# Six half-bank output slots, straight-line code and a third index buffer in the edge loop of a graph layer on Trainium2

## What is computed

```python
def reference(x, src, dst, edge_weight, ...):          # x [6250, 256], 100000 edges sorted by dst
    xn = layernorm(x)
    agg = segment_sum(edge_weight[:, None] * xn[dst], src, 6250)
    x = x + (agg @ gnn_W.T + gnn_b) + linear_attention(xn)
    h = layernorm(x)
    for e in range(8):                                  # top 2 of 8 experts, softmax of their scores
        out += combine[:, e] * (relu(h @ W1[e].T + b1[e]) @ W2[e].T + b2[e])
    return x + out
```

## Time and profile before

| | before |
|---|---|
| device time, 3 runs | 2444.96 to 2448.07 us, median 2445.28 |
| the profiled execution | 2440.68 us, span of its instructions 2438.9 us |
| mean granted TensorE clock | 0.824 of full speed |
| PE busy | 1657.1 us (68%) |
| DVE busy | 1435.1 us (59%) |
| ACT busy | 1321.6 us (54%) |
| POOL busy | 1394.9 us (57%) |
| the edge loop: first to last gather | 327.0 to 1687.9 us |

### The profile page before, as it was taken

The page is one execution under the profiler, slowest core; times in us unless marked ns, Lnnn a source line. Parts: engine busy times, 40 slices in busy tenths (PEclk is TensorE's granted clock), DMA queues, the critical chain, the costliest instruction groups (busy, mean ns, idle before and its releaser), DMA issues. The chain is left out here.

```text
span 2438.9 us, 52037 instructions
## 1 busy us (share of the span) xinstructions
PE 1657.1 (68%) x13448; PEld 1188.0 (49%) x13448; DVE 1435.1 (59%) x3494; ACT 1321.6 (54%) x4250; POOL 1394.9 (57%) x1333
## 2 busy tenths in 40 slices
PE   6876446666666566666665444444639999999998
PEld 3465424444444445545442111122327777777776
DVE  7998535555555565555555554555855555555554
ACT  6454335555555455555555555554645665666665
POOL 3688846666666666666666666665404444444444
PEclk8999868888888687888986656566559999999999
DMA  4022144444444443333333334442612233233222
GB/s 145 15 85 71 55 130 133 131 125 131 129 126 128 132 118 101 99 99 99 101 90 90 88 89 119 148 136 77 205 26 43 48 50 49 45 50 49 46 49 32
DMA packets 139601, 224.62 MB, mean 92 GB/s; under 512 B 33398, under 2 KB 94016, under 8 KB 139298
## 3 DMA queue, kind: packets, MB, share of 16 engines
q0 software_dynamic: 67040, 146.22, 23.5%
q1 hardware_dynamic: 66022, 69.75, 9.6%
q10 hardware_dynamic: 6364, 6.40, 0.8%
HBM read 181.40 MB, written 41.82 MB: 92 GB/s over the span
## 5 line engine op out<-in xcount | busy, mean ns | idle before, releaser
L961 POOL DMA_INDIRECT misc<-z_d,consts x902 | 861.0, 955 | 520.0 <-remote 251.1
L1206 DVE SCALAR_TENSOR_TENSOR acc<-ps,consts,acc 128x256 f32 x902 | 434.2, 481 | 545.6 <-remote 485.4
L1286 PE MATMUL ps<-misc 128*128 128x256 f16 x565 | 185.5, 328 | 295.4 <-DVE acc L1206 150.0
L1790 ACT ACTIVATE misc<-ps,misc 128x128 f32<-128x128 f32 x840 | 240.1, 369 | 237.8 <-PE ps L1755 166.1
L985 ACT ACTIVATE rec<-rec,misc 128x128 f16<-128x128 f16 x674 | 229.2, 392 | 210.8 <-DVE rec L1067 145.3
L1831 POOL DMA_INDIRECT out<-misc,pos x105 | 166.2, 1583 | 289.0 <-ACT misc L1855 253.3
L1755 PE MATMUL ps<-misc,big 128*128 128x128 f16 x1680 | 327.2, 220 | 0.0
L1753 PE MATMUL ps<-misc,big 128*128 128x128 f16 x1680 | 326.8, 220 | 0.1
L1754 PE MATMUL ps<-misc,big 128*128 128x128 f16 x1680 | 326.5, 219 | 0.0
L985 ACT ACTIVATE misc<-rec,misc 128x128 f16<-128x128 f16 x678 | 229.1, 391 | 171.6 <-DVE rec L1067 128.2
L1770 PE MATMUL ps<-big,rec 128*128 x840 | 319.7, 381 | 0.0
(11 more groups left out here) (336 smaller groups left out, 3835.6 us busy)
## 6 DMA issues: line engine op xcount, KB each, us to landing
big<-in_w2T SPq DMA_DIRECT2D x60, 256.0 KB
misc<-z_d,consts POOLq DMA_INDIRECT x902
big<-xT_d SPq DMA_DIRECT2D x98, 128.0 KB
big<-in_w1T SPq DMA_DIRECT2D x32, 256.0 KB
tok_d<-misc SPq DMA_DIRECT2D x50, 132.0 KB, 2.8
xT_d<-misc SPq DMA_DIRECT2D x49, 128.0 KB
z_d<-misc SPq DMA_DIRECT2D x49, 128.0 KB
acc<-in_x SPq DMA_DIRECT2D x1, 6144.0 KB
```

Source lines behind the costliest of these rows:

```text
L961: e.indirect_dma_start(out=rows[k], out_offset=None, in_=c.z_d, in_offset=bass.IndirectOffsetOnAxis(ap=idx[u][:, k:k + 1], axis=0)).then_i ...
L1206: e.scalar_tensor_tensor(out=rows_of, in0=out_ps[t % BG], scalar=c.gain, in1=rows_of, op0=ALU.mult, op1=ALU.add).then_inc(s_add[k], 1)
L1286: e.matmul(o, w[:, 0, :], rows[k][:, 0:D], start=True, stop=False)
L1790: l = e.activation(hidden[:, m, :], h_ps[u][:, m, :], ACT.Relu, bias=b1x[u][:, m:m + 1])
```

## The change

Three edits, all in `graph`. **Slots:** `BG` goes from 3 to 6, and two tiles share a bank, each in one half; PE and DVE now wait once for two tiles. PE asks before an even tile t for the addition of tile t-5 (so both tiles that had the bank before are added), and DVE asks before it adds an even tile t for the product of tile t+1. **Straight line:** PE, ACT and DVE run `for at in range(LOOPS)`, with no loop of the sequencers and constants in all counts. **Third buffer:** `idx` and `near` have three buffers, and `fetch` copies round q+2 while ACT is in round q; rounds 0 and 1 are copied before the first turn.

```diff
-UG, HG, OG, BG, LEAD = 12, 8, 4, 3, 6
+UG, HG, OG, BG, LEAD = 12, 8, 4, 6, 6
...
-        c.idx = [k.take(UG, I32) for _ in range(2)]
+        c.idx = [k.take(UG, I32) for _ in range(3)]
...
-    near = [matrix(misc.take(UG * 3), UG, 3) for _ in range(2)]
+    near = [matrix(misc.take(UG * 3), UG, 3) for _ in range(3)]
...
-    out_ps = [c.bank[k][:, 0:D] for k in range(BG)]
+    out_ps = [c.bank[k // 2][:, k % 2 * D:k % 2 * D + D] for k in range(BG)]
...
-            def fetch(q, u):
-                if not first(q) and not (isinstance(q, int) and q == 1):
-                    e.wait_ge(s_mm[UG - 1], q - 1)
+            def fetch(q):
+                u = q % 3
+                if q >= 3:
+                    e.wait_ge(s_mm[UG - 1], q - 2)
...
                     if t % UG == 6:
-                        if t // UG == 0:
-                            fetch(j * 2 + 1, 1)
-                        elif at < LOOPS - 1:
-                            fetch(j * 2 + 2, 0)
+                        if j * 2 + t // UG + 2 < turns:
+                            fetch(j * 2 + t // UG + 2)
...
-            fetch(0, 0)
-            loops(e, turn)
+            fetch(0)
+            fetch(1)
+            for at in range(LOOPS):
+                turn(at, at)
...
-                    e.wait_ge(s_mm[k], q + 1)
+                    if t % 2 == 0:
+                        e.wait_ge(s_mm[k + 1], q + 1)
                     e.scalar_tensor_tensor(out=rows_of, in0=out_ps[t % BG], scalar=c.gain, in1=rows_of,
                                            op0=ALU.mult, op1=ALU.add).then_inc(s_add[k], 1)
...
-                wait(e, s_add[(k - BG) % UG], j * 2 + (t - BG) // UG + 1)
+                if t % 2 == 0:
+                    wait(e, s_add[(k - BG + 1) % UG], j * 2 + (t - BG + 1) // UG + 1)
```

More of the change, by code:

```diff
@@ L858, in wait @@
             e.wait_ge(sem, n)
-    def loops(e, body):
-        for at, end in ((0, 1), (1, M2), (M2, B0 - 1), (B0 - 1, B0), (B0, B0 + 1), (B0 + 1, M9), (M9, LAST), (LAST, LAST + 1),
-                        (LAST + 1, L0), (L0, L0 + 4), (L0 + 4, L1), (L1, L1 + 3), (L1 + 3, L1 + 4), (L1 + 4, LOOPS - 1),
-                        (LOOPS - 1, LOOPS)):
-            if end - at == 1:
-                body(at, at)
-            else:
-                with e.Fori(at, end) as j:
-                    body(j, at)
     def weight(layer, n, m):
@@ L985, in weigh @@
                     e.activation(hot[t % HG][:, half, :], same[t % OG], ACT.Copy,
-                                 scale=near[t // UG][:, t % UG, 1 + half:2 + half]).then_inc(s_hot, 1)
+                                 scale=near[n // UG % 3][:, t % UG, 1 + half:2 + half]).then_inc(s_hot, 1)
             def features(h, k, s):
```

8 lines of the change are left out of this document (4 added, 4 removed).

## The result

The changed kernel takes 2427.41 us (median of 4 runs, 2424.52 to 2429.18), the kernel before 2445.52 us beside it: ratio 0.9924, 95% interval 0.9911 to 0.9936. Forecast was 2382 us. It is faster, but by 18 us and not by 63. A second series gave 0.9935 (0.9918 to 0.9952).

What follows compares the result with a forecast made beforehand. The prediction took the edge loop to be bound by POOL's gather steps plus 232 us of stalls behind PE's late signals. Slots 63 us less, straight line and third buffer nothing: 2382 us, with 2310 to 2470 for 8 in 10.

Steps and rivals of the forecast that it cites:

- What bounds the kernel now: Edge loop: POOL's gathers step at 1.252 us; the other 232 us are stalls, ended by late signals of PE's products.
- what length a run of gathers has follows from counts: Edge loop: a release frees three signals, so buys three gathers; six slots would buy three more, 2.5 after the pairs' cost.
- the whole term of the slots: Edge loop, BG 3 to 6: longer runs, fewer stalls; 25, 23 and 15 us less in three stretches, 63 us in sum.
- Bounds: Limits on the slots' gain: nothing if stalls only move, 30 us if each left grows to 2.90 us, at most all 232 us.
- the sum at today's prices: Slots' gain with each stretch's stalls kept at their present length: 63 us less, chosen because it used each stretch's own row.
- for it: Evidence for the forecast: products and signals microseconds apart, and PE's 249 us behind the additions being a wait for slots.
- Straight line: Turns of PE, ACT and DVE written out: engines 53% to 58% busy only meet waits sooner; costed at nothing.
- Third buffer: Index copies for POOL: it had waited 2.0 us for ACT's copies; gain 0 to 2 us, taken as 0.
- C: Rival: PE's signals held back in number, or pairs eat the gain; stalls keep their count, 2425 to 2455 us; chance 0.15.
- D: Rival: straight code's added instruction traffic, 0.68 MB, stops engines and costs time, 2449 to 2499 us; chance 0.18.
- B: Rival: runs of gathers so long that hardly a stall is left, POOL's 1.253 us the bound; about 2300 us; chance 0.10.

Runs made afterwards that it cites:

- e2_slots: The kernel before with only six half-bank slots and paired waits, loops and two index buffers kept: 2446.86 us, ratio 1.0001.
- e3_line_third: The changed kernel with three slots again, a bank each and a wait a tile; straight code and third buffer kept: 2431.62 us, ratio 0.9946.
- e15_paced_again: The changed kernel's edge loop alone, with a small POOL fill behind each gather, on a chip with late signals: 1.494 us a tile.
- e7_alone_deep: The changed kernel's edge loop alone, with twelve slots for six, twelve weighed tiles for eight, comparison ten tiles ahead for six: 1.454 us a tile.
- e8_alone_half: The changed kernel's edge loop alone, each gather fetching half of each row, the second product made from the same half: 1.461 us a tile.
- e1_line: The kernel before with only PE's, ACT's and DVE's turns written out; three slots, two index buffers: 2433.16 us, ratio 0.9936.
- e5_line_dve: The kernel before with VectorE's 38 turns alone written out; ScalarE and TensorE keep loops: 2434.28 us, ratio 0.9974.
- e14_push_again: The changed kernel's edge loop alone, with three extra 128-column matmuls behind each product, on a chip with late signals: 1.490 us a tile.
- e6_alone: The changed kernel with the edge loop alone in its stage; features, attention, expert-weight splitting and block loads left out: 1.461 us a tile.
- e16_sp_again: The changed kernel's edge loop alone, rows brought by SyncE's plain transfers instead of POOL's gathers, on a chip with late signals: 1781.13 us in all.
- e12_push: The changed kernel with four slots on two banks and three extra matmuls behind each product, on the fast chip: 2213.75 us, ratio 1.0044.

## Why the prediction was wrong, point by point

**What bounds the kernel now** held where it read rows. The loop is paced by steps of 1.252 us and 232 us of silences, and these end when TensorE's late signals come out. The chip without late signals supports the reading: in the kernels traced there the silences are all but gone, and the kernel before, which was not traced there, is 240 us shorter.

**The step that failed** is "what length a run of gathers has follows from counts", with the sentence that a release lets out three signals and so buys three gathers, and from it the whole term of the slots: -25, -23 and -15 us in three stretches, -63 in sum. The measured term is nil, both with loops (e2_slots, ratio 1.0001) and with straight code (e3_line_third beside the change: 1342.9 and 1344.2 us). I took the price of a silence as fixed and its number as what the buffers set. It is the other way about: on the chips with late signals the mean step is 1.45 to 1.51 us in all these kernels, whatever the buffers, and they only change how the difference to POOL's own step is cut into silences. e15_paced_again shows it most plainly, since there the gap between gathers takes over about half of the silences' time with the mean nearly where it was; e7_alone_deep, with twice the slots and a longer lead, and e8_alone_half say the same. My "for it" was PE's 249 us behind the additions: they did fall, to 157.9 us (and to 151.8 us with three slots, e3_line_third), and the wait at L1263 grew from 103.7 to 137.3 us. A wait that ends last in a group of waits is not yet the one that sets the pace.

**Bounds.** "A stall may keep its number and only change its place (nothing gained)" was one of the ends that I named, and it is what happened. I took the sum at today's prices in its place because it used more rows, not because a row spoke for it.

**Straight line**, costed at nothing, is the whole gain within what can be told: 1344.4 us in e1_line for 1360.9, 16.5 us, and 14.7 us less than e2_slots on its own chip. The reasoning was that an engine busy 58% of the stage only meets its wait sooner, and that step failed as well. VectorE's part is some 6 us (e5_line_dve); the rest comes with TensorE's and ScalarE's. Why it gains is open, with two candidates. One is the count of instructions (3256 fewer on the page of e1_line), by a price that all engines' instructions would share. The other is stops in the loops. The Trainium skill (Runtime: NRT & Kernel Launch, Instruction fetch mechanics) gave the sign, by its rule that a taken branch out of the fetched window stops an engine. The trace of the kernel before has stops behind branches, as that rule would have it, and they are small: VectorE's next instruction starts 0.2 to 0.3 us after each of the 23 branches back, and 0.03 us after the six that leave a loop, and TensorE's branches back take 215 ns in place of 83:

```profile
L868 PEldq COMPARE_BRANCH  x29: 83/215/231, 409.1 to 1610.6; - x29
```

That is 3 to 5 us on either engine if nothing of it is hidden. VectorE's register instructions over 200 ns were 24 before and none after, and their times add up to 15.9 us, as much as the whole gain; but e5_line_dve has none of them either and gained 6 us. No run keeps the count and takes the stops away. That stops are not the whole story is suggested by e14_push_again, which has no branch more than e6_alone and is 26.6 us longer.

**Third buffer** at nothing: right with three slots (e3_line_third against e1_line, 1342.9 and 1344.4 us). With six slots and two buffers POOL waited 11.1 us for ScalarE's copies (e2_slots) in place of 2.0, as the prediction supposed, and in the changed kernel it waits for none; what that is worth in time was not measured apart.

**Rivals.** C came nearest: stalls keep their count (173 for 174) and the time was put at 2425 to 2455, which holds 2427. It had 0.15, and its reason ("held back in number", or the pairs eat the gain) is not what was found. D, instruction traffic, is out, since the stage got shorter. The queues that bring instructions, from 327 to 1695 us,

```profile
q8 instruction: 37, 0.61, 0.2%
q14 instruction: 66, 0.54, 0.1%
```

carry 1.15 MB where the earlier trace rows had 0.52: 0.63 MB more, near the 0.68 reckoned. The size of the traffic was right, and its price was less than what the straight code gains. B's number is what one chip gives without any change at all (2206 us). That the range for 8 in 10 holds 2427 us is owed to the weight given to C, not to the mechanism forecast. The later stages kept their time, as forecast.

**What stays open.** Shown is that on the chips where the kernel before takes 2426 to 2447 us, TensorE's signals are held up to microseconds while POOL gathers, that plain transfers of as many bytes do not do it, that an idle engine's empty instructions are held up in the same stretch, and that on one chip TensorE's signals are prompt. Argued, with a fit of 4.5 to 5.9 ns an instruction that one chip's three kernels do not follow, and with one direct test (3 to 4 ns), is that all instructions share a path whose rate sets the pace.

Instructions alone can't fill such a path: e16_sp_again went through 13,537 of them in 664.5 us, 20.4 a microsecond, without a late signal, and the kernel before through 22,183 in 1360.9 us, 16.3. Taken at 5 ns each, an estimate from these fits, they leave about 1.39 us a tile in the kernel before (24.6 instructions a tile) as in e6_alone (15.2), so most of the step would be the gather's own.

What the path is, no run here shows. The Trainium skill (NOTIFIC — the notification-queue block, Interfaces) says of the block that writes the records of instructions and semaphores that its back-pressure can stall an engine when an internal FIFO fills. The missing releasers ("remote") on the chips with late signals would fit it, but every execution here was a recorded one, so it stays a guess. If it were so, the gain of the straight code would be a gain of recorded executions. What the change is worth on a chip with prompt signals was not measured either; with POOL at its own 1.25 us a step there, I would expect nothing.

## What to carry to other kernels

When three engines and a queue wait for each other in a ring, a count of buffers need not tell how much waiting there is; here it only told how the waiting was cut up. Change the spacing of the fastest one first (here a 0.17 us fill behind each gather): if the mean stays where it was, something other than the buffers sets it. Price instructions off the critical path by a kernel that has more of them, not by the idle time beside them. And look at the kernel before on more than one chip before explaining its idle time by its program.

## What the runs showed of the hardware

Five series were run where the kernel before took 2426 to 2448 us, one on a chip where it took 2206. The difference lies in the stage in which POOL issues 902 gathers of 128 rows: it took 1134.8 us in e12_push on the fast chip and 1342.9 to 1360.9 us in the whole kernels on chips where the kernel before takes 2441 us or more, and what follows it took 750 to 758 us on all. In one kernel, VectorE's additions that had to wait came 0.20 us after the recorded end of their product on the fast chip and 5.9 us after it on another (medians; longest 0.57 and 11.2 us). Plain transfers of the same bytes, two tiles in 1.5 us, made no addition wait for a product on either. The branch of an idle engine, 45 ns by its median in any case, took up to 1401 ns while the gathers ran. The gathers' own instruction was 0.95 us on both kinds of chip.
